# Context rows turned by transposing DMAs between two Pool copies, and two of 32 row maxima moved into the exponentials

## The reference

```python
def xcond(q, k, v, k_length):           # q = layernorm(x), k = v = context
    s = SCALE * jnp.log(k_length)[:, None, None, None]
    attn = softmax(s * jnp.einsum('bhdq,bhdk->bhqk', qh, kh))
    return jnp.einsum('bhqk,bhdk->bhdq', attn, vh)
x = x + xcond(layernorm(x), ctx, ctx, itok)
x = x + ffn(layernorm(x), ...)          # routed experts + 0.2 * (gelu(x@sw1+sb1)@sw2+sb2 + gelu(x@swd)@swu)
```

## Time and profile before

| | us |
|---|---|
| median of 3 runs | 1346.81 |
| lowest and highest | 1346.71, 1350.07 |
| profiled execution | 1353.0 |
| its span, first to last instruction | 1351.2 |
| TensorE busy | 1305.0 (97%) |
| VectorE busy | 839.0 (62%) |
| ScalarE busy | 704.5 (52%) |
| Pool busy | 250.8 (19%) |
| mean granted TensorE clock | 0.991 |

### The profile page before, as it was taken

The page is one execution under the profiler, slowest core; times in us unless marked ns, Lnnn a source line. Parts: engine busy times, 40 slices in busy tenths (PEclk is TensorE's granted clock), DMA queues, the critical chain, the costliest instruction groups (busy, mean ns, idle before and its releaser), DMA issues.

```text
span 1351.2 us, 26893 instructions
## 1 busy us (share of the span) xinstructions
PE 1305.0 (97%) x11055; PEld 950.2 (70%) x11072; DVE 839.0 (62%) x1408; ACT 704.5 (52%) x1056; POOL 250.8 (19%) x219
## 2 busy tenths in 40 slices
PE   5788999999999999999999999999999999999997
PEld 2143646556464737375788889999999988888895
DVE  7777768778778787765552844728456284472730
ACT  4757675757676666673332533535344353442521
POOL 4540000000001041433200311203012030120012
PEclk9899999999999999999999999999999999999999
DMA  9514141222356223324826757767576675767413
GB/s 273 183 55 125 33 110 48 83 67 71 79 72 70 84 67 102 98 52 72 266 94 134 196 141 188 170 141 197 145 201 147 139 198 142 186 145 152 95 25 40
DMA packets 182572, 165.08 MB, mean 122 GB/s; under 512 B 104889, under 2 KB 125513, under 8 KB 182450
## 3 DMA queue, kind: packets, MB, share of 16 engines
q1 hardware_dynamic: 170162, 138.15, 39.0%
q0 software_dynamic: 12288, 25.21, 10.9%
HBM read 109.47 MB, written 34.15 MB: 106 GB/s over the span
## 4 chain that ended last, share of the span: by engine, by line
PE 86%; DVE 4%; ACT 4%; issue 3%; POOL 1%; DMA 0%; POOLq 0%; ACTq 0%; DVEq 0%
PE banks L1821 25%; PE banks L1851 24%; PE banks L1755 11%; PE banks L1737 10%; PE banks L1677 4%; PE banks L1657 4%; PE banks L1625 3%; DVE rowmax L1281 2%; ACT hidden L1058 1%; ACT QS L1045 1%; PE banks L1711 1%; PE banks L1686 1%; PE banks L1862 1%; PE banks L1723 1%; POOL w1l L942 1%
## 5 line engine op out<-in xcount | busy, mean ns | idle before, releaser
L1851 PE MATMUL banks<-hidden,w2h 128*128 128x0 bf16 x2048 | 306.1, 269 | 0.0
L1058 ACT ACTIVATE hidden<-banks,scales 128x512 f32<-128x512 f32 x256 | 171.1, 686 | 101.5 <-PE banks L1657 86.4
L1851 PEld LDWEIGHTS banks<-hidden,w2h 128*128 128x128 bf16 x2048 | 198.6, 98 | 20.5
L1281 DVE TENSOR_REDUCE rowmax<-banks 128x1 f32<-128x512 f32 x256 | 172.5, 684 | 40.3 <-PE banks L1625 38.3
L1851 PE MATMUL banks<-hidden,w2l 128*128 128x0 bf16 x1024 | 192.3, 269 | 0.0
L1432 DVE TENSOR_TENSOR w1l<-stage,w1h 128x2048 bf16<-128x2048 f32 x32 | 73.2, 2291 | 186.3 <-ACT w1h L1135 186.3
L1755 PE MATMUL banks<-w2h,hidden 128*128 128x512 bf16 x512 | 184.3, 379 | 0.0
L1152 ACT ACTIVATE hf<-banks,b1cols 128x640 f32<-128x640 f32 x128 | 101.1, 790 | 123.1 <-PE banks L1821 107.7
L1163 ACT ACTIVATE yT<-banks 128x640 uint16<-128x640 uint16 x56 | 36.3, 701 | 215.3 <-PE banks L1851 215.3
L1821 PE MATMUL banks<-eth,w1h 128*128 128x0 bf16 x1024 | 133.0, 273 | 0.0
L1821 PE MATMUL banks<-eth,w1l 128*128 128x0 bf16 x1024 | 132.9, 273 | 0.0
(11 more groups left out here) (198 smaller groups left out, 1970.4 us busy)
## 6 DMA issues: line engine op xcount, KB each, us to landing
stage<-in_L_ffn_w SPq DMA_DIRECT2D x64, 1024.0 KB
split_parts<-hidden SPq DMA_DIRECT2D x16, 512.0 KB, 5.8
QS<-split_parts SPq DMA_DIRECT2D x48, 128.0 KB, 2.7
KS<-split_parts SPq DMA_DIRECT2D x48, 128.0 KB, 3.1
xin<-in_x SPq DMA_DIRECT2D x16, 256.0 KB, 3.7
cin<-in_ctx SPq DMA_DIRECT2D x16, 256.0 KB, 3.6
out_rows<-xin SPq DMA_DIRECT2D x16, 256.0 KB, 2.0
normed_rows<-x2r SPq DMA_DIRECT2D x16, 256.0 KB, 3.2
```

Of the source, the lines that this page charges most:

```text
L1058: ac.activation(prob[n % NPH], bank(score_bank[unit]), ACT.Exp, scale=scales[:, g // 2:g // 2 + 1]).then_inc(s_exp, 1)
L1281: dv.reduce_max(rowmax[g % 2][:, i:i + 1], bank(score_bank[unit]), X_AXIS).then_inc(s_max, 1)
L1851: issued = mm(bank(b0 + j)[:, skips[j]:CAP].shape_from_register(used_cols(e, j)), w[:, fb, rows], of_choice(a[:, fb, :], j, skips[j]).shap ...
```

## The change

For windows 1 to 6 (groups 4 to 15) `turn_v` is replaced by two units. `split_v` at steps 0 and 6 of the up pass: Pool copies the 512 f32 of each context row as 1,024 two-byte halves into two planes, low halves and high halves, in one instruction, and SyncE issues two transposing DMAs, one for each plane, into a second tile. `join_v` at steps 5 and 11: Pool, once both DMAs have landed and the values of the group before in that buffer are done, copies the turned planes, interleaved again, into `VT`. Groups 0 to 3 are turned as before. The two tiles share memory with `b2f` and `wuf`. `LATE` goes from 8 to 10: the last ten scores of an odd group, not eight, are taken beside the exponentials, now from the first one on (i = 0), and the up pass takes 14 scores, not 16. `load` and `c_load` stay at step 3.

```diff
-LATE = 8
+LATE = 10
@@ exponentials_and_down
-                if i >= (UNITS - EARLY if k else 2 if w else 1):
+                if i >= (UNITS - EARLY if k else 0 if w else 1):
                     next(score, None)
                 if k == 0:
-                    if i == (LATE + 2 if w else UNITS - 3):
+                    if i == (LATE if w else UNITS - 3):
                         add("parts", g + 1)
-                    elif i > (LATE + 3 if w else UNITS - 3):
+                    elif i > (LATE + 1 if w else UNITS - 3):
                         next(rows, None)
-                    one_of(side, 1 if k == 0 and w and i < LATE else 2)
+                    one_of(side, 1 if k == 0 and w and i < 8 else 2)
@@ up_pass
-            if more and n in (2, 3):
+            if more and w == 0 and n in (2, 3):
                 add("turn_v", a + n)
-                if a + 4 < GROUPS and n == 3:
-                    add("load", a + 4)
-                    add("c_load", a + 4)
+            if more and w and n in (0, 6):
+                add("split_v", a + 2 + n // 6)
+            if more and w and n in (5, 11):
+                add("join_v", a + 2 + n // 6)
+            if n == 3 and a + 4 < GROUPS:
+                add("load", a + 4)
+                add("c_load", a + 4)
@@ tiles
+        turned_v = wuf_turned[:, :].bitcast(U16).rearrange("p (a c) -> p a c", a=2)
+        planes = b2f_planes[:, :].bitcast(U16).rearrange("p (a c) -> p a c", a=2)
@@ sync_program
+                elif kind == "split_v":
+                    g = unit[1]
+                    sp.wait_ge(s_vt, g + 1)
+                    sp.wait_ge(s_vtc, g)
+                    for a in range(2):
+                        dma(turned_v[:, a, :].rearrange("p (t c) -> p t c", c=P), planes[:, a, :], transpose=True).then_inc(s_vturn, 16)
@@ pool_program
+                elif kind == "split_v":
+                    g = unit[1]
+                    pool.wait_ge(s_c[g % 2], 16 * (g // 2 + 1))
+                    if g == NS:
+                        pool.wait_ge(s_b2, 1)
+                    else:
+                        pool.wait_ge(s_vturn, 16 * 2 * (g - NS))
+                    gp.tensor_copy(planes, cin[g % 2][:, :].bitcast(U16).rearrange("p (c a) -> p a c", a=2)).then_inc(s_vt, 1)
+                elif kind == "join_v":
+                    g = unit[1]
+                    pool.wait_ge(s_vturn, 16 * 2 * (g - NS + 1))
+                    pool.wait_ge(s_pv, QT * (g - 1))
+                    if g == NS:
+                        pool.wait_ge(s_wuc, 1)
+                    gp.tensor_copy(VT[g % 2][:, :].bitcast(U16).rearrange("p (c a) -> p a c", a=2), turned_v).then_inc(s_vtc, 1)
@@ pe_program, rows
-                        pe.wait_ge(s_vtc, g + 2)
+                        pe.wait_ge(s_vtc, min(g + 2, NS))
```

More of the change, by code:

```diff
@@ L482, in build @@
         wdh, wdl = sb("wdh", [P, KB, WIDE], BF16), sb("wdl", [P, KB, WIDE], BF16)
-        wuf, wus = sb("wuf", [WIDE, D], F32), sb("wus", [P, D], BF16)
+        wuf_turned, wus = sb("wuf_turned", [P, D], F32), sb("wus", [P, D], BF16)
+        wuf = wuf_turned[0:WIDE, :]
+        turned_v = wuf_turned[:, :].bitcast(U16).rearrange("p (a c) -> p a c", a=2)
         hidden = sb("hidden", [P, 2 * FB * SLOTS], BF16)
@@ L500, in build @@
         sb1rows, sb1cols = sb("sb1rows", [FB, P], F32), sb("sb1cols", [P, FB], F32)
-        b2f = sb("b2f", [E + 1, D], F32)
+        b2f_planes = sb("b2f_planes", [P, D], F32)
+        b2f = b2f_planes[0:E + 1, :]
+        planes = b2f_planes[:, :].bitcast(U16).rearrange("p (a c) -> p a c", a=2)
         b2parts = sb("b2parts", [E + 1, 3, D], BF16)
@@ L615, in build @@
         s_stack = [sem(f"s_stack{i}") for i in range(NS)]
-        s_vt, s_vtc = sem("s_vt"), sem("s_vtc")
+        s_vt, s_vtc, s_vturn = sem("s_vt"), sem("s_vtc"), sem("s_vturn")
         s_score, s_max, s_ms, s_rows, s_row = (sem(n) for n in ("s_score", "s_max", "s_ms", "s_rows", "s_row"))
```

## The result

| us | before | after |
|---|---|---|
| median, runs of one chip | 1348.44 (6) | 1357.53 (6) |
| lowest and highest | 1346.71, 1351.07 | 1354.35, 1358.33 |
| profiled execution, its span | 1353.0, 1351.2 | 1356.3, 1354.5 |

The change makes the kernel slower: the ratio after to before is 1.0058, with an interval of 1.0047 to 1.0070, or +7.8 us. I had forecast 1347.9, +1.1 us; the median lies 1.5 us above the range.

A forecast was written before the change was run, and what follows sets the result against it. TensorE was taken as the bound, with VectorE a quarter microsecond from it at two places in each pass. Head 0.7 plus middle 6.0 minus removed 5.6 gave +1.1 us on 1346.8: 1347.9 us, range 1341.0 to 1356.0.

The forecast's parts named there:

- Removed: Up passes of windows 1 to 6: eight transposes leave TensorE, 0.93 us each window, 5.6 us saved; ScalarE's evictions count nothing.
- Moved: Two scores go from up pass to exponentials: same TensorE cost, 1.4 us of maxima fit VectorE's idle time; cost nothing.
- buys no margin: Up pass loses 1.4 us of VectorE work, but in its last three steps, behind both narrow places.
- SyncE and the DMAs: 24 transposing DMAs land well before the exponentials need them; x load about 3 us later; all costed at nothing.
- The copy's length: Each Pool split or join, called c, taken as 1.0 us, between 0.94 and 2.3.
- the estimate of 0.88: Copy length in us from the Trainium skill's 1.03 cycles per element at 1.2 GHz; the sum would end 1.9 us lower.
- The middle: Mid up pass: join and split hold VectorE 1.4 us, less 0.20 margin: 1.2 us of TensorE, five windows, 6.0 us.
- The head: Up pass start: split follows VectorE's subtraction, delays its sum 0.40 us, less 0.28: 0.12 us, six windows, 0.7 us.
- the margin of 0.28: At the up pass's head, how many us later VectorE's maximum may come before TensorE stands still for its PSUM bank.
- the base: Median of the kernel before, 1346.8 us, on which the forecast difference of +1.1 was set.
- The rival that I had for the slower side: Mid-pass, same port lock, copies above 1.19 us: +9.1 us (1355.9) at 1.5, +21.9 (1368.7) at 2.3; chance 0.18.
- 16c - 9.3: Cost in us of head and middle holds over all windows, c being copy length; each 0.1 us is worth 1.6.

The follow-up runs named there:

- versions on ScalarE: Kernel after with eight late scores and each window's four copies on ScalarE instead of Pool: 1342.63 us beside 1349.43 before, ratio 0.9951, windows 72.36 us.
- placed copies: Kernel after with eight late scores, x load ahead of splits, each Pool copy waiting for a VectorE idle stretch: 1345.35 us, ratio 0.9957 to before, windows 72.37.
- the head split behind the denominators: Kernel after, each window's first split also waiting for VectorE's first denominator transpose: windows 78.31 us against 74.81; with the x load ahead of the split, 73.75.
- The run with the order forced: Kernel after, each window's first split also waiting for the VectorE subtraction that it had overtaken: windows 74.10 us against 74.81.

## Why the prediction was wrong, and where it was right

By the trace, the windows grew by 7.7 us where I had +1.1. The 6.6 us, by the steps of the forecast:

- **Removed, 5.6 us: nearly right.** The versions on ScalarE and with placed copies give 0.90 us a window, 5.4 in all; 0.2 us of the miss.
- **Moved, nothing: wrong by 0.17 to 0.22 a window,** 1.0 to 1.3 us. I asked where the moved maxima go and found room for them. I did not ask what the score had covered at the place that it left: ScalarE's copy of `x2t`, for which the gate matmul then waits. The sentence that the move "buys no margin" held; that it costs nothing did not.
- **SyncE and the DMAs, nothing: right.** But I read the later x load as harmless without its margin; the head split behind the denominators shows what is lost with it, 4.6 us a window (78.31 against 73.75), of which 1.7 are the lower clock behind the standstill.
- **The copy's length, 1.0 us: right for the split** (1.03), low for the join (1.33); the estimate of 0.88 is too low for both. The longer join hardly shows in the middle: it also started earlier against VectorE's addition than I had drawn (231.0 as the subtraction ahead of it ended, with the addition due at 231.70), and held it by 0.49 against my 0.4; the split held the next subtraction by 0.83 against my 1.0.
- **The middle, 1.2 us: right,** by its mechanism and its size (1.21), window 6 without it as said.
- **The head, 0.12 us: the step that failed.** What I had wrong is the order in which the two engines get the ports there. The head is 0.98 in windows 2 to 4, about 1.45 in window 5, and some 1.0 in window 6: 3 x 0.86 + 1.33 + 0.9, about 4.8 of the 6.6 us. The forecast said "The split starts there, waits for VectorE's subtraction of 216.61 to 217.22". In the trace the split starts 0.6 us after the store (its row gives 0.87, and rows overlap), about when the subtraction does, and takes the ports. Then the delay is nearly the whole copy, 1.26 us, less the margin of 0.28, and not the 0.40 that is left behind an instruction that comes first. The run with the order forced gives 74.10, and 0.26 to 0.35 for the head. Only window 1, where TensorE shows no wait at the head, came out near what I had (+0.46 against +0.39), and that is luck: its first split finds no store ahead of it and runs at 133.21, 8.8 us before the pass begins, and the moved scores' 0.22, which I had not seen, stands in for the 0.12.

The remaining quarter microsecond is window 0, which I had left out. The turning there is the old one, but the moved scores and the first split reach into it: the gate's wait is 0.48 us instead of 0.26, and the split of 133.21 lies beside VectorE's norm (1.06 us instead of 0.53), for which TensorE then waits 0.23. This window also moves by more than that between executions: it took 65.02 and 66.40 us in two of the same kernel (copies on ScalarE), and in the second one the granted clock was 0.50 from 127.2 to 130.6 us. The last 3 us between 1347.9 and 1357.5 are the base: the three runs that I took it from had a median of 1346.8, six have 1348.4, and the two medians lie 1.3 us further apart than the ratio says. On the base that I used, the measured +7.8 would be 1354.6, inside my range; the change itself is what I had wrong, +1.1 against +7.8.

The rival that I had for the slower side was the same lock with a slow copy. The side was right and its cause was not: the split was as fast as I took it, and the join's 0.33 us more hardly showed. My formula 16c - 9.3 hid the assumption, because it let only c vary; the order at the head is worth 1.26 - 0.54 = 0.7 us a window, and the formula has no term for it. The sum should have been done for both orders.

What stays open: why Pool's copy comes first at the ports, when its row starts 0.09 us after VectorE's in windows 2 to 4 and 0.44 us after it in window 5. The rows don't show a request, only a start and an end. In both cases the copy stands right behind the issue of the store, whose row VectorE's instruction overlaps; whether that matters was not tried. The same store without a copy behind it held neither the cast nor the subtraction before (0.42 and 0.69). Nor did I try the change with only the odd group's copies moved.

## What to carry to other kernels

When an idle engine takes over work, ask which resource it shares with a busy one, and place its instructions by semaphore in stretches where the busy one doesn't want that resource; the same four copies cost 2.2 us of TensorE a window when they start as soon as they can, and nothing when they are placed or given to ScalarE. Where two instructions that share something can start within half a microsecond of each other (0.09 and 0.44 here), price both orders. Of an instruction that is moved away, look at what it covered where it stood, and of a wait that is added, at the DMAs queued behind it. A kernel whose TensorE hardly waits loses more by a long standstill than its length: the clock behind it counts too.

## What the runs showed of the hardware that I had not expected

- The start of a row does not tell who has the shared ports. VectorE's subtraction, listed 0.09 us ahead of Pool's copy, was the one held: 1.95 us instead of 0.69. So was a cast listed 0.44 us ahead, 2.06 us instead of 0.41.
- A Pool memset, which reads nothing, left VectorE instructions with two SBUF inputs alone (0.68 and 0.42 us, free) but held a cast of 512 f32 elements with one input: 2.04 us instead of 0.41, over Pool's store issue and the memset behind it.
- The same copy of 1,024 two-byte elements takes 1.03 us on Pool and 1.04 on ScalarE when the interleaved side is read, and 1.33 and 1.36 when it is written. Beside the 24 copies on ScalarE no VectorE instruction took longer than it does otherwise.
- After TensorE stood still for 3.68 us, or for 2.00 us in window 5 of the kernel with each copy twice, the granted clock was 0.50 for 3.4 us and then 1.00 again. After the waits of up to 1.29 us in windows 1 to 6 of after it stayed at 1.00. In window 0 waits of 0.50, 0.95 and 1.56 us follow each other; of two executions of the kernel with the copies on ScalarE, the clock fell behind them in one and not in the other.
